# Routed experts of a transformer block: four result buffers with a signal each, and the residual added by TensorE while the four places are summed in halves of 256 columns

## The reference

```python
logits = x @ router_w                                  # 8192 tokens, 64 experts
probs_all = jax.nn.softmax(logits, axis=-1)
top_p, top_i = jax.lax.top_k(probs_all, K)             # K = 4
...
buf = jnp.zeros((E, CAP, h)).at[expert_id, pos].set(perm_x)    # CAP = 128
h1 = jnp.einsum('ech,ehf->ecf', buf, w1)
g = jax.nn.silu(h1[..., :I]) * h1[..., I:]             # I = 64
y = jnp.einsum('eci,eih->ech', g, w2)
perm_y = y[expert_id, pos]
perm_probs = probs.T.reshape(-1)[order]
out = jnp.zeros((T, h)).at[token_idx].add(perm_y * perm_probs[:, None])
```

## Time and profile before

| | us |
|---|---|
| median of 3 runs | 4823.22 |
| lowest and highest | 4818.7 and 4835.57 |
| the profiled execution | 4828.26 |
| its span, first to last instruction | 4826.5 |
| expert stage, first load to last of POOL's sends | 4617.2 to 4726.4 |
| combining stage, first load to last store issued | 4733.4 to 4822.7 |

### The profile page before, as it was taken

How to read it: one execution, slowest core, us unless ns; L and a number is a source line. 1 busy time by engine, 2 the same in 40 slices (tenths; PEclk the granted TensorE clock), 3 DMA queues, 4 the chain that set the end, 5 groups by cost and what they waited for, 6 DMA issues and landing times. The chain is left out here.

```text
span 4826.5 us, 84373 instructions
## 1 busy us (share of the span) xinstructions
PE 3253.8 (67%) x23496; PEld 1981.1 (41%) x23496; DVE 3560.6 (74%) x13313; ACT 2188.5 (45%) x3945; POOL 1388.4 (29%) x1176
## 2 busy tenths in 40 slices
PE   4777769998886999977777566655555555532144
PEld 1222224445665444446666444433333343321133
DVE  7999966666886565658888788688888888853348
ACT  5999963334554444434444333344444444410020
POOL 5777740001001222220000322311111111157751
PEclk9999989998998999988998899855556655555575
DMA  2000031000000000000000000000000000020026
GB/s 62 4 4 4 4 128 84 0 0 9 7 6 23 1 1 0 0 9 9 10 10 9 4 0 0 7 4 3 3 3 3 3 3 3 2 95 14 1 77 188
DMA packets 110377, 95.82 MB, mean 20 GB/s; under 512 B 64780, under 2 KB 95705, under 8 KB 107006
## 3 DMA queue, kind: packets, MB, share of 16 engines
q1 hardware_dynamic: 86654, 78.97, 5.7%
q0 software_dynamic: 14336, 10.87, 0.7%
q10 hardware_dynamic: 9216, 4.20, 0.3%
HBM read 55.57 MB, written 57.97 MB: 24 GB/s over the span
## 5 line engine op out<-in xcount | busy, mean ns | idle before, releaser
L366 PE MATMUL PS<-IDENT,a_T 128*77 128x128 f32 (+1 forms) x3584 | 630.5, 326 | 20.8 <-ACT a_xw L455 15.3
L929 ACT ACTIVATE l_H<-l_H 128x2048 f32<-128x2048 f32 (+2 forms) x256 | 597.7, 2717 | 2.9 <-POOL l_H L981 2.7
L366 PEld LDWEIGHTS PS<-IDENT,a_T 128*77 128x77 f32 (+1 forms) x3584 | 543.6, 185 | 59.2 <-issue 33.9
L981 POOL TENSOR_TENSOR l_H<-l_feat,l_text 128x4096 f32<-128x4096 f32 x64 | 450.6, 7041 | 131.2 <-PE PS L885 130.5
L474 ACT ACTIVATE a_Pr<-PS 77x512 f32<-77x512 f32 (+1 forms) x640 | 377.0, 592 | 145.6 <-PE PS L366 139.8
L885 PE MATMUL PS<-l_H,l_wide 128*32 128x512 f32 (+1 forms) x2560 | 332.5, 596 | 163.6 <-ACT l_H L929 163.5
L552 POOL TENSOR_TENSOR a_T<-a_mx,a_T 128x616 f32<-128x616 f32 x128 | 155.6, 1217 | 903.7 <-DVE a_mx L632 903.5
L1003 DVE TENSOR_TENSOR l_H<-PS,l_text 128x2048 f32<-128x2048 f32 (+1 forms) x192 | 412.0, 2147 | 2.1 <-ACT l_text L956 2.1
L404 PE MATMUL PS<-a_Wo,a_OT 128*128 128x128 f32 x384 | 111.5, 380 | 417.1 <-DVE a_vaug L704 308.6
L460 ACT ACTIVATE a_yT<-PS 128x128 f32<-128x128 f32 x192 | 53.3, 277 | 684.3 <-PE PS L321 684.3
L541 POOL TENSOR_TENSOR X<-X,a_bo 128x128 f32 (+1 forms) x192 | 87.6, 457 | 829.4 <-DVE a_y L589 829.4
(11 more groups left out here) (287 smaller groups left out, 8182.9 us busy)
## 6 DMA issues: line engine op xcount, KB each, us to landing
expert_shares<-e_zero SPq DMA_DIRECT2D x16, 1024.0 KB, 22.0
e3c_four<-expert_shares SPq DMA_DIRECT2D x64, 256.0 KB, 3.3
e3x_xin<-expert_rows SPq DMA_DIRECT2D x32, 200.0 KB, 2.5
expert_rows<-e_zero SPq DMA_DIRECT2D x6, 1024.0 KB, 8.7
a_cT<-in_ctxT SPq DMA_DIRECT2D x128, 38.5 KB, 1.8
X<-in_x SPq DMA_DIRECT2D x8, 512.0 KB, 7.2
e_w<-in_L_ffn_w SPq DMA_DIRECT2D x1, 4096.0 KB, 13.5
expert_rows<-e3r_row,e3r_rows_at POOLq DMA_INDIRECT x256, 2.1
```

The lines of the kernel that those rows point to most:

```text
L366: last = pe.transpose(PS[0:keys, 4 + g % 2, j * S:(j + 1) * S], T[:, u, c:c + keys], m.IDENT[:, :])
L929: act.activation(cells, cells, ACT.Tanh).then_inc(q[f"tanh{part}"], 1)
L981: pool.tensor_tensor(H[:, a, lo * S:hi * S].rearrange("p (t f) -> p t f", f=S), bcast(feat[:, a, :], 1, hi - lo), bcast(text[:, a, lo:hi], ...
```

## The change

In the expert stage res gets four buffers, v = s % 4, and sent four semaphores, so that DVE waits for the shares of step s - 4 instead of s - 2; find_places gets a wait for the same semaphore before it overwrites share_at. In the combining stage PE adds X to the far product by a second product, of the identity matrix and X, into the same PSUM bank; base goes. The four places are summed by two additions: two, 256 columns, then sums, 128 columns, one step later; done, now from PSUM and sums, comes two steps later. The signal four comes from two, pair from sums, and PE waits for sum in place of base. DVE's loop is written out in full.

```diff
-            res = sc("res", [CAP, 2, 2 * D])
+            res = sc("res", [CAP, 4, 2 * D])
...
-                            in_=res[:, u, e * D:(e + 1) * D], in_offset=None,
-                            bounds_check=PLACES - 1, oob_is_err=False).then_inc(q[f"sent{u}"], 16)
+                            in_=res[:, v, e * D:(e + 1) * D], in_offset=None,
+                            bounds_check=PLACES - 1, oob_is_err=False).then_inc(q[f"sent{v}"], 16)
                 run_fours(pool, step, 0, 0, NP)
-                for u in range(2):
-                    pool.wait_ge(q[f"sent{u}"], NP // 2 * 32)
+                for v in range(4):
+                    pool.wait_ge(q[f"sent{v}"], NP // 4 * 32)
...
                     dve.wait_ge(q["coded"], q.nth("coded", i))
+                    if past(i, 4):
+                        dve.wait_ge(q[f"sent{v}"], c * 32)
                     dve.tensor_scalar(share_at[:, v, :], place[:, u, :], float(PLACES), None, ALU.add) \
                         .then_inc(q["meta"], 1)
...
                         dve.wait_ge(q["down"], q.nth("down", s))
-                        if past(s, 2):
-                            dve.wait_ge(q[f"sent{u}"], (2 * c + v // 2) * 32)
+                        if past(s, 4):
+                            dve.wait_ge(q[f"sent{v}"], c * 32)
                         dve.wait_ge(q["meta"], q.nth("meta", s))
                         for e in range(2):
-                            dve.tensor_scalar(res[:, u, e * D:(e + 1) * D], PS[:, 4 + u, e * D:(e + 1) * D],
+                            dve.tensor_scalar(res[:, v, e * D:(e + 1) * D], PS[:, 4 + u, e * D:(e + 1) * D],
...
             def _(pe):
                 for s in range(B):
                     if past(s, 4):
-                        pe.wait_ge(q["base"], q.nth("base", s, 4))
+                        pe.wait_ge(q["sum"], q.nth("sum", s, 4))
                     half = slice(s % 2 * E, (s % 2 + 1) * E)
                     pe.matmul(PS[:, s % 4, 0:D], wfT[half, s // 2 * S:(s // 2 + 1) * S], lastT[half, :],
-                              start=True, stop=True) \
+                              start=True, stop=False)
+                    pe.matmul(PS[:, s % 4, 0:D], m.IDENT[:, :], m.X[:, s, :], start=False, stop=True) \
                         .then_inc(q["far"], 1)
 
             @block.vector
             def _(dve):
                 def step(s, v, c):
-                    if real(s):
-                        dve.wait_ge(q["far"], q.nth("far", s))
-                        dve.tensor_tensor(base[:, v, :], PS[:, v, 0:D], seq(m.X, s), ALU.add).then_inc(q["base"], 1)
+                    if s < B:
                         dve.wait_ge(q[f"c{v}"], c * 16 + 16)
-                        dve.tensor_reduce(sums[:, v, :], four[:, v, :].rearrange("p (k d) -> p d k", d=D), AX, ALU.add) \
+                        dve.tensor_tensor(two[:, v, :], four[:, v, 0:2 * D], four[:, v, 2 * D:4 * D], ALU.add) \
                             .then_inc(q["four"], 1)
-                    if real(s - 1):
+                    if 0 <= s - 2:
+                        w = (v - 2) % 4
+                        if past(s - 2, 4):
+                            dve.wait_ge(q[f"out{w}"], (c - (0 if v > 1 else 1)) * 16)
+                        dve.wait_ge(q["far"], q.nth("far", s - 2))
+                        dve.wait_ge(q["pair"], q.nth("pair", s - 2))
+                        dve.tensor_tensor(done[:, w, :], PS[:, w, 0:D], sums[:, w, :], ALU.add).then_inc(q["sum"], 1)
+                    if 0 <= s - 1 < B:
                         w = (v - 1) % 4
-                        if past(s - 1, 4):
-                            dve.wait_ge(q[f"out{w}"], (c - (0 if v else 1)) * 16)
                         dve.wait_ge(q["four"], q.nth("four", s - 1))
-                        dve.wait_ge(q["base"], q.nth("base", s - 1))
-                        dve.tensor_tensor(done[:, w, :], base[:, w, :], sums[:, w, :], ALU.add).then_inc(q["sum"], 1)
-                run_fours(dve, step, 0, 1, B)
+                        dve.tensor_tensor(sums[:, w, :], two[:, w, 0:D], two[:, w, D:2 * D], ALU.add) \
+                            .then_inc(q["pair"], 1)
+                for s in range(B + 2):
+                    step(s, s % 4, s // 4)
```

More of the change, by code:

```diff
@@ L1771, in layer3_experts @@
             "skeytop", "at", "wf", "wfTps", "wfT", "passed", "held", "scat0", "scat1", "in0", "in1", "in2", "in3", "xT", "xTs",
-            "up", "gate", "hid", "hidT", "hidTs", "down", "rank", "coded", "meta", "ress", "sent0", "sent1",
-            "last", "lastin", "far", "c0", "c1", "c2", "c3", "four", "base", "sum", "out0", "out1", "out2", "out3",
+            "up", "gate", "hid", "hidT", "hidTs", "down", "rank", "coded", "meta", "ress", "sent0", "sent1", "sent2", "sent3",
+            "last", "lastin", "far", "pair", "c0", "c1", "c2", "c3", "four", "sum", "out0", "out1", "out2", "out3",
             "loaded"])
@@ L2228, in layer3_experts @@
             four = inner.enter_context(nc.sbuf_tensor("e3c_four", [S, 4, K * D], F32))
+            two = inner.enter_context(nc.sbuf_tensor("e3c_two", [S, 4, 2 * D], F32))
             sums = inner.enter_context(nc.sbuf_tensor("e3c_sums", [S, 4, D], F32))
-            base = inner.enter_context(nc.sbuf_tensor("e3c_base", [S, 4, D], F32))
             done = inner.enter_context(nc.sbuf_tensor("e3c_done", [S, 4, D], F32))
```

## The result

The median of 20 runs fell from 4827.77 to 4815.98 us, a ratio of 0.9978 with a 95% interval of 0.9971 to 0.9984: faster by 11.8 us, a third of the 34.6 that were forecast, and above the range given (4776 to 4806). The profiled execution has a span of 4810.4 us, against 4826.5 before.

What follows compares the result with a forecast made beforehand. It saw the expert stage held by DVE's wait for landing shares, the combining stage by DVE. Savings of 16 + 18.6 = 34.6 us from the 4823.2 us median gave a forecast of 4789 us, range 4776 to 4806.

Steps and rivals of the forecast that it cites:

- The old wait: Expert stage: DVE's wait for the shares of two steps before, median 1.04 us, longest 2.79; forecast to go.
- 1.28 a send: Expert stage: POOL's time per indirect DMA, two a step or 2.56 us, forecast as the new bound; 80.6 us for 63 intervals.
- the new wait: Expert stage: find_places waits for share_at of four steps before; loop 2.2 us a step, under POOL's 2.56, so no cost.
- the allowance: Expert stage: 0.9 us left for wake-ups where POOL is still short, taking the saving from 16.9 to 16 us.
- Rival 3: Expert stage: sent wait replaced, not removed, or PE's 1.2 GHz lasts; 9 us saved, not 16; 4796 to 4805; chance 0.13.
- DVE's step of 0.73: Combining stage: DVE needs 0.33 + 0.20 + 0.20 = 0.73 us a step, below DMA.
- DMA's step of 1.04: Combining stage: DMA becomes the bound at 1.04 us a step instead of 1.335, saving 18.6 us.
- bound of 1.10: Combining stage: upper end of the forecast's 1.00 to 1.10 us a step; forecast's chance 0.56.
- Four passes of 128 rows start 0.85 us before the next four: under 1.0: Combining stage: PE's step with the added X product, claimed to cost nothing unless it ceases to overlap.
- 74.5 us forecast for the stage: Combining stage: its whole time after the forecast saving of 18.6 us.
- Rival 4: Combining stage: switching 64-row and 128-row weights stops loads overlapping matmuls; PE 3.0 us a step, 89 us slower, 4912; chance 0.03.
- PE's wait for sum of four steps back: Combining stage: wait moved from base to sum; four steps, about 4 us, available for 1.06, so hidden.

Runs made afterwards that it cites:

- e1: Expert stage as changed (four res buffers), combining stage as in the kernel before; 4888.28 us on chip D, ratio 1.0022 to the kernel before.
- e3: Changed kernel without PE's product of IDENT and X, so the residual is left out; 4869.72 us on chip D, ratio 0.9996 to the kernel before.
- e5: Changed kernel with the far product on 128 rows too, lastT zero in the other half; 4877.60 us on chip D, ratio 0.9999 to the kernel before.
- e5b: Changed kernel with all combining-stage weights of 128 rows, lastT padded with zeros; 4797.94 us on chip B, ratio 0.9932 to the kernel before.
- e8: e5 with eight buffers and signals for the e3c_four loads in place of four; 4860.07 us on chip E, ratio 0.9976 to the kernel before.
- b0b_before: The kernel before, nothing changed, run again on chip F; 4884.28 us in one run.
- b0_before: The kernel before, nothing changed, run again on chip B; 4823.12 us in one run.

## Why the prediction was right, and where it failed

- Expert stage: right, in mechanism and size. The old wait went, POOL became the bound at 1.28 a send, the new wait was hidden behind it, and 17.2 us came for 16 forecast (16.9 before the allowance). Rival 3 didn't occur. But this holds for chips A and B (e1's expectation of 17 us less turned into 11.6 more on D); that the same step could cost time elsewhere, no row of before on A said.
- DVE's step of 0.73: right. Where it waits for nothing, as in a piece of e3, its additions start at 4821.78, 4821.98, 4822.18 and 4822.51: 0.20, 0.20 and 0.33 apart.
- DMA's step of 1.04: near, and never in force in the changed kernel. Once PE was out of the way, four buffers gave 1.056 to 1.130, all above the forecast, e5 and e5b beyond its bound of 1.10 too, eight 1.03 to 1.05; the landing rose from 3.3 to 3.5 to 3.9, as the forecast had it (about 3.5). By the 358 GB/s of the Trainium skill (page "DMA: Bandwidth & Descriptors", section "Specifications") a step would be 0.92, an estimate. The runs didn't get there: e8 moved 317 GB/s over 40 us, at share 1.00.
- PE: the step that failed. "Four passes of 128 rows start 0.85 us before the next four: under 1.0" priced the far product by a row of another shape. Two of the four passes have weights of 64 rows, and what decides is the change of size, 0.30 us each, twice a step: 1.45 in place of 0.85. That is 0.41 above the 1.04 of DMA, and 64 times that, 26 us, less the 3.3 us by which PE starts ahead of the first addition, is about the gap between 74.5 us forecast for the stage and 97.2 measured.
- Rival 4 named just this mechanism and was given 0.03. Its price, 3.0 a step, was twice too high: it let every pass pay a load and a matmul in full (0.75), while a change drains PE once per product. At 0.30 a change it would have read 1.45, and a time near the one measured. "Against it: 128-row passes ran 0.21 apart" was no evidence against a change of size, since those passes had none between them. None of the rows read had one, but the trace of before did. In its cross attention, at the upper clock level (1.00), products with weights of 32 rows and of 128 rows follow each other:

```profile
1145.17 0.31 PEld L311 LDWEIGHTS PS<-a_kblk,a_qT 32*128 32x128 f32 x8
1145.90 0.14 PEld L321 LDWEIGHTS PS<-IDENT,a_y 128*128 128x128 f32 x1 [0.42 <-issue]
```

The load behind the change stands 0.42 us with no engine waited for, the sign that the changed kernel shows ahead of each product. It starts 0.07 us before the end of the pass ahead of it, as the loads behind changes there do; between passes of one size in e5b the next starts 0.21 before.

- PE's wait for sum of four steps back was hidden, as forecast (0.5 us in 2 waits from 4720 to 4800), and that didn't help: buffers cover a late start, not a rate.

## What to carry to other kernels

Where products alternate between weights of 64 and of 128 rows, count a drain for every change; group products by size, or pad the smaller weights with zeros to 128 rows, which here cost no time and gave 16.7 us by the medians on B. Before moving work to an engine that looks idle, price the sequence it will run, not each instruction by a row taken between its like. And time a change on more than one chip: a gain of 0.2% here was a loss of 0.3% elsewhere.

## What the runs showed of the hardware that I had not expected

- A change between 64-row and 128-row fp32 weights costs PE 0.30 us at the lower clock level, with one PSUM bank or two (stage 97.2 and 97.0 us).
- The granted clock stayed at 0.50 (1.2 of 2.4 GHz) through 60 us in which the profile shows PE busy without a gap, while in e5b, busy 29.3 of 40 us in passes of one size, its mean was 0.79, and a pass at the upper level took 0.11 us (two from 4759.98 to 4760.21). "Busy" counts the drains in the former: its rows of 0.79 us start 0.72 apart, with a stand of 0.2 ahead of each weight load.
- Three of the five chips that the record numbers take 40 to 50 us more for the same kernel. Of the 61 us between the spans of b0b_before (4882.5) and b0_before (4821.4), 47 lie in the routing stage and 6 in the expert stage, both with indirect DMAs, where engines wait for signals whose releaser the profile can't place, up to 25 us at a time. What holds them is open.
